# Int8 linear layer of a transformer kernel: rounding, transposes and product by halves of the tokens, casts placed earlier, second half scaled on ScalarE

## The chip, the cores and the metric

The kernel runs on one core of a Trainium2 chip. The metric is the device time of one execution in microseconds, lower is better.

## What is computed

The reference is four layers, each of an attention and a feed-forward part with a layernorm ahead and a residual sum behind. It works on 16 sequences of 64 tokens with 128 features. The change lies in the feed-forward part of the second layer (counted from 0, layer 1), an int8 product, cut here to what matters:

```python
def _xla_quantized_matmul(x2d, weight_q, weight_scale):
    amax = jnp.max(jnp.abs(x2d), axis=-1, keepdims=True)
    x_scale = jnp.maximum(amax, EPS) / 127.0
    x_q = jnp.clip(jnp.round(x2d / x_scale), -128, 127).astype(jnp.int8)
    acc = jax.lax.dot_general(x_q, weight_q, (((1,), (1,)), ((), ())), preferred_element_type=jnp.int32)
    return acc.astype(jnp.float32) * x_scale * weight_scale[None, :]
...
x = x + _L1_xattn_ref(_layernorm(x, axis=-1), ctx_1024, ctx_1024, ...)     # channel attention
x = x + _L1_ffn_ref(_layernorm(x, axis=-1), weight_q, weight_scale, bias)  # product above, + bias
x = x + _L2_xattn_ref(ctx_1024, ctx_1024, _layernorm(x, axis=-1), ...)     # deformable attention
```

## The kernel before

The 1024 tokens are eight tiles of 128 (tokens on the partitions, 128 features along a row). The residual stream is `x_tm`, its layernorm `h_tm`, the transposed layernorm `h_fm`. There are no loops at run time: each stage writes out, engine by engine, a fixed list of instructions with waits on semaphores, and the lists of one engine follow each other in the order of the source. So the order on an engine is the order in the text, and an instruction behind a wait stands until the wait is met.

The stages around the change, in order:

- `channel_attention(2)` (from L1118). On TensorE the last product (L1172) is two halves of 64 matmuls; VectorE stands at `wait_ge(y_ps, k + 1)` (L1198), adds each half to `x_tm` (L1202) and takes statistics (L251).
- `int8_linear(3)` (L1294 to L1389). A layernorm of all tiles: VectorE makes five tiles of `h_tm` (L277), ScalarE three (L292). VectorE casts the integer weights to bf16 (`wq8b`, L1312) and the identity matrix (`ident_b`, L1313), finds the largest magnitude of each token (L1315), the scale `xs` and its reciprocal (L1316, L1317), multiplies (L1318), rounds by adding and taking away a large constant (L1319), and clips into bf16 (`xq`, L1320). TensorE transposes the eight tiles into PSUM bank 4 (L1354), ScalarE copies them out in one instruction (`xT`, L1380), TensorE multiplies tile by tile by `wq8b` into banks 2 and 3 (L1360) and counts up `y_ps` after each half. Meanwhile VectorE adds the bias to `x_tm` (L1321). Then for each half k it multiplies the product by the token's scale into `y` (L1325), by the weight's scale (L1330), adds it to `x_tm` (L1331) and takes statistics. Half 0's layernorm is begun by `first_norm.moments` (L336, L338), its square root is ScalarE's (`first_norm.root`, L342 and L344), and its factors and two of its four tiles are done on VectorE (L349, L350, L365) between L1325 and L1330 of half 1; ScalarE does the two other tiles (L358). `second_norm` does the same for half 1.
- Around the int8 product, TensorE fills waits with matmuls whose result nobody reads (`stay_busy`, L241). Behind the product it transposes nine blocks of another layer's weights (L1367) into banks 6, 7 and 5, makes the last layer's keys in banks 0 and 1 (L1371), runs two more `stay_busy` matmuls and then transposes half 0 of `h_tm` (`first_norm.turn`, L376). ScalarE copies the weights' transposes out (L1383), then does the root, the keys' first half (L1255), its tiles of `h_tm` (L358), the keys' second half, and `h_fm` (L382).
- `deformable(4)` starts from `h_fm`: queries (L1457, L1465) and offsets (L1477) on TensorE, copies on ScalarE (L1548, L1554), positions on VectorE (L1577 and on), first for half 0 and then for half 1.

`dve_link` lets VectorE wait for the end of the instruction just issued. `REST` counts DMAs of inputs, all issued at the kernel's start.

## Time and profile before

| | us |
|---|---|
| median of 3 runs | 476.1 |
| the 3 runs | 476.1, 476.27, 471.72 |
| profiled execution, its own time | 471.51 |
| profiled execution, span of its trace | 469.7 |
| PE, DVE, ACT, POOL busy in the span | 393.7, 363.0, 247.9, 110.7 |
| mean granted TensorE clock | 0.967 |

The span runs from the first to the last instruction. PE is TensorE (PEld its weight loads), DVE is VectorE, ACT is ScalarE, POOL is GpSimd. Times within the trace count from the start of the span. A timeline line gives start, duration, engine, source line, operation, tensors, shapes and count; merged instructions stand on one line, and in brackets is how long the engine had been idle and what released it. In the chain of waits a line gives start, duration and what was running; its pieces do not overlap.

### The profile page before, as it was taken

How to read it: one execution, taken by the hardware profiler on the slowest of the kernel's cores; microseconds unless marked ns; L12 is line 12 of the kernel's file. 1: busy time of each engine (PE TensorE's matmuls, PEld its weight loads, DVE VectorE, ACT ScalarE, POOL GpSimd, SP SyncE). 2: the span in 40 equal slices, each digit the busy share in tenths (PEclk: the TensorE clock that was granted, in tenths of full speed). 3: DMA queues.
4: the chain of work that ended last, by engine and by line, in shares of the span. 5: the costliest groups of instructions: out<-in, count | busy, mean ns of one | idle time of the engine just before them, and what ended most of it. 6: DMA issues, size and time to landing. Idle time of an engine off the chain costs nothing.

```text
span 469.7 us, 8627 instructions
## 1 busy us (share of the span) xinstructions
PE 393.7 (84%) x3391; PEld 259.2 (55%) x3391; DVE 363.0 (77%) x805; ACT 247.9 (53%) x429; POOL 110.7 (24%) x95
## 2 busy tenths in 40 slices
PE   4999889999999988786887888899999995678056
PEld 1656556566666667553454446575667763553045
DVE  3799656648544587889878898999898789777985
ACT  3764853324223334457787884855866334435931
POOL 3200000005990001006995345210410133000000
PEclk9999999999999999989999999999999998979659
DMA  7880000000000000026000003000000000000001
GB/s 241 354 298 3 2 1 0 2 0 1 0 1 0 1 3 2 0 98 262 2 1 0 3 1 68 1 1 2 0 1 1 2 0 1 3 0 0 1 0 46
DMA packets 11084, 16.51 MB, mean 35 GB/s; under 512 B 5274, under 2 KB 9764, under 8 KB 10148
## 3 DMA queue, kind: packets, MB, share of 16 engines
q1 hardware_dynamic: 10756, 15.17, 9.2%
q10 hardware_dynamic: 288, 0.79, 0.5%
q8 instruction: 27, 0.44, 0.4%
q14 instruction: 13, 0.11, 0.1%
HBM read 15.43 MB, written 0.52 MB: 34 GB/s over the span
## 4 chain that ended last, share of the span: by engine, by line
PE 48%; DVE 32%; ACT 11%; issue 6%; DMA 1%; POOL 1%; DVEq 0%; ACTq 0%
PE ps L808 7%; PE ps L813 7%; PE ps L847 7%; PE ps L2075 4%; PE ps L241 3%; DVE arena L613 2%; PE ps L2065 2%; DVE arena L616 2%; DVE arena L1862 2%; PE ps L1714 2%; DVE stats L251 2%; PE ps L2102 1%; DVE arena L635 1%; DMA ctx_fm<-in_ctx_fm 1%; PE ps L2617 1%
## 5 line engine op out<-in xcount | busy, mean ns | idle before, releaser
L926 DVE SCALAR_TENSOR_TENSOR arena<-ps,cols,arena 128x512 f32<-128x512 f32 x40 | 29.8, 750 | 42.3 <-PE ps L813 38.0
L822 ACT ACTIVATE arena<-ps,cols 128x512 f32<-128x512 f32 x40 | 27.4, 687 | 63.9 <-PE ps L808 63.9
L241 PE MATMUL ps<-const 128*128 128x256 f32 x152 | 40.1, 412 | 7.4 <-ACT arena L2658 4.4
L847 PEld LDWEIGHTS ps<-weights,arena 128*128 128x128 f32 x320 | 38.5, 192 | 8.1 <-issue 8.0
L1862 DVE TENSOR_SCALAR arena<-ps 128x512 f32<-128x512 f32 x56 | 36.4, 684 | 7.3 <-PE ps L1700 3.5
L847 PE MATMUL ps<-weights,arena 128*128 128x128 f32 x320 | 39.2, 276 | 0.2 <-DVE x_tm L915 0.2
L241 PEld LDWEIGHTS ps<-const 128*128 128x128 f32 x152 | 29.8, 205 | 16.4 <-ACT arena L2658 4.7
L813 PE MATMUL ps<-h_fm,weights 128*128 128x512 f32 x80 | 37.7, 593 | 0.7 <-DVE arena L926 0.7
L808 PE MATMUL ps<-h_fm,weights 128*128 128x512 f32 x80 | 37.7, 594 | 0.6 <-ACT h_fm L382 0.6
L2065 PE MATMUL ps<-h_fm,weights 128*128 128x512 f32 x64 | 30.3, 606 | 2.7 <-ACT arena L2443 1.8
L1700 PE MATMUL ps<-l2buf,picks_b 128*128 128x256 bf16 x160 | 25.5, 275 | 6.5 <-DVE arena L1862 4.7
L2075 PEld LDWEIGHTS ps<-weights,arena 128*128 128x128 f32 x256 | 29.4, 192 | 2.6 <-issue 2.6
L2075 PE MATMUL ps<-weights,arena 128*128 128x128 f32 x256 | 30.0, 275 | 0.9 <-DVE x_tm L2287 0.9
L813 PEld LDWEIGHTS ps<-h_fm,weights 128*128 128x128 f32 x80 | 15.1, 190 | 20.2 <-issue 18.2
L1714 PE MATMUL ps<-arena,kexp 128*32 128x320 f32 x256 | 20.5, 438 | 5.3 <-ACT l2buf L1805 3.9
L1021 POOL TENSOR_TENSOR wn<-wn,winv 128x1152 f32<-128x1152 f32 x1 | 2.1, 2127 | 88.8 <-DVE winv L1011 88.8
L2443 ACT ACTIVATE arena<-ps 128x512 f32<-128x512 f32 x32 | 18.0, 597 | 9.2 <-PE ps L2065 9.1
L915 DVE SCALAR_TENSOR_TENSOR x_tm<-ps,arena,x_tm 128x128 f32<-128x128 f32 x80 | 22.4, 342 | 0.3 <-DVE stats L251 0.2
L1700 PEld LDWEIGHTS ps<-l2buf,picks_b 128*128 128x128 bf16 x160 | 12.6, 99 | 16.9 <-DVE arena L1862 10.0
L2065 PEld LDWEIGHTS ps<-h_fm,weights 128*128 128x128 f32 x64 | 11.2, 189 | 17.7 <-issue 10.2
L808 PEld LDWEIGHTS ps<-h_fm,weights 128*128 128x128 f32 x80 | 13.7, 191 | 10.4 <-issue 9.6
L2226 POOL TENSOR_TENSOR arena<-arena 128x1024 f32<-128x1024 f32 x5 | 11.5, 2298 | 31.7 <-DVE arena L2325 31.7
(391 smaller groups left out, 880.5 us busy)
## 6 DMA issues: line engine op xcount, KB each, us to landing
weights<-in_moe_w SPq DMA_DIRECT2D x2, 2048.0 KB, 9.9
weights<-in_moe_w SPq DMA_DIRECT2D x3, 1280.0 KB
l2buf<-in_picks SPq DMA_DIRECT2D x1, 1664.0 KB, 7.9
rows<-in_rows SPq DMA_DIRECT2D x1, 1024.0 KB, 13.1
x_tm<-in_x SPq DMA_DIRECT2D x2, 256.0 KB, 5.0
ctx_fm<-in_ctx_fm ACTq DMA_DIRECT2D x1, 512.0 KB, 5.7
ctx_tm<-in_ctx SPq DMA_DIRECT2D x1, 512.0 KB, 14.0
mats<-in_mats SPq DMA_DIRECT2D x1, 512.0 KB, 14.4
```

Source lines behind the costliest of these rows:

```text
L241: PE.matmul(ps[:, bank, 0:256], ident, const[:, 0:256], start=True, stop=True)
L808: PE.matmul(ps[:, k, :], w1[:, e, P * k:P * k + P], h_fm[:, t], start=True, stop=True)\
L813: PE.matmul(ps[:, 2 + k, :], w2[:, e, P * k:P * k + P], h_fm[:, t], start=True, stop=True)\
L822: AC.activation(silu[:, k, :], ps[:, k, :], ACT.Silu, bias=bias_col(0, e, k)).then_inc(silu_ok, 1)
L847: ins = PE.matmul(ps[:, 4 + u % 2, P * t:P * t + P], glu[:, u % 2, k, P * t:P * t + P], w3[:, e, k, :], start=(k == 0), stop=(k == 1))
L915: ins = V.scalar_tensor_tensor(out=x_tm[:, j], in0=ps[:, 4 + u % 2, P * t:P * t + P], scalar=gates[:, j, e:e + 1], in1=x_tm[:, j], op0=ALU ...
L926: V.scalar_tensor_tensor(out=glu[:, u % 2, k, :], in0=ps[:, 2 + k, :], scalar=bias_col(1, e, k), in1=silu[:, k, :], op0=ALU.add, op1=ALU.m ...
L1700: ins = PE.matmul(ps[:, m % 3, 256 * i:256 * i + 256], picks_b[:, 2 * c + i, :], ixm[:, hg, 256 * half:256 * half + 256], start=True, stop ...
L1714: ins = PE.matmul(ps[32 * hl:32 * hl + 32, 4 + par, 0:NK * S], kvc[:, j, 4 * hg + hl, :], hats[:, u % 2, NK * hl:NK * hl + NK, S * (2 * i ...
L1862: V.tensor_scalar(hat_rows(u, c), ps[:, m % 3, :], 0.0, 1.0, ALU.max, ALU.min).then_inc(near_ok, 1)
L2065: PE.matmul(ps[:, n % 3, :], m2w1[:, e, P * k:P * k + P], h_fm[:, 0:T2], start=True, stop=True)\
L2075: ins = PE.matmul(at_ps, hid[:, e % 2, k, P * j:P * j + P], m2w2[:, e, k, :], start=(k == 0), stop=(k == 3))
```

## The change

The two casts are issued in the channel attention, ahead of VectorE's wait for the first half of its last product. The clip (L1320), the transposes, the copy out of PSUM and the product are each issued in two halves of four tiles; the second half's transposes go to bank 5. ScalarE, which before had only the copy to do here, waits for the product's second half and multiplies it, tile by tile, by the token's scale `xs`; VectorE keeps this step for the first half alone, and ahead of L1330 of half 1 it waits for ScalarE (`xT_ok` at 6: two copies and four scalings).

```diff
@@ channel_attention, VectorE
                 dve.wait_ge(dve_chain, biased)
+                dve.wait_ge(rest_in, REST)
+                V.tensor_copy(wq8b[:], wq8[:])
+                V.tensor_copy(ident_b[:], ident)
                 for k in range(2):
                     t = slice(4 * k, 4 * k + 4)
                     dve.wait_ge(y_ps, k + 1)
@@ int8_linear, VectorE
-                dve.wait_ge(rest_in, REST)
-                V.tensor_copy(wq8b[:], wq8[:])
-                V.tensor_copy(ident_b[:], ident)
                 wait_h_tm(dve)
...
-                V.tensor_scalar(xq, t, -128.0, 127.0, ALU.max, ALU.min).then_inc(xq_ok, 1)
+                for k in range(2):
+                    r = slice(4 * k, 4 * k + 4)
+                    V.tensor_scalar(xq[:, r], t[:, r], -128.0, 127.0, ALU.max, ALU.min).then_inc(xq_ok, 1)
...
-                    dve.wait_ge(y_ps, k + 1)
-                    dve_link(V.tensor_tensor(y[:, r], ps[:, 2 + k, :].rearrange("p (j c) -> p j c", j=4),
-                                             over(xs[:, r], 2, D), ALU.mult))
+                    if k == 0:
+                        dve.wait_ge(y_ps, 1)
+                        dve_link(V.tensor_tensor(y[:, r], ps[:, 2, :].rearrange("p (j c) -> p j c", j=4),
+                                                 over(xs[:, r], 2, D), ALU.mult))
                     if k == 1:
                         first_norm.factors(dve)
                         first_norm.apply_on_dve(dve, (0, 1))
+                        dve.wait_ge(xT_ok, 6)
@@ int8_linear, TensorE
-                pe.wait_ge(xq_ok, 1)
-                for j in range(NT):
-                    ins = PE.transpose(tp[:, P * j:P * j + P], xq[:, j], ident_b[:])
-                ins.then_inc(xT_ps, 1)
-                pe.wait_ge(xT_ok, 1)
                 for k in range(2):
+                    pe.wait_ge(xq_ok, k + 1)
+                    tp = ps[:, 4 + k, :].bitcast(BF16)
+                    for j in range(4):
+                        ins = PE.transpose(tp[:, P * j:P * j + P], xq[:, 4 * k + j], ident_b[:])
+                    ins.then_inc(xT_ps, 1)
+                for k in range(2):
+                    pe.wait_ge(xT_ok, k + 1)
                     for j in range(4):
                         i = 4 * k + j
@@ int8_linear, ScalarE
-                act.wait_ge(xT_ps, 1)
-                AC.activation(xT, ps[:, 4, :].bitcast(BF16), ACT.Copy).then_inc(xT_ok, 1)
+                for k in range(2):
+                    act.wait_ge(xT_ps, k + 1)
+                    AC.activation(xT[:, 512 * k:512 * k + 512], ps[:, 4 + k, :].bitcast(BF16)[:, 0:512], ACT.Copy)\
+                        .then_inc(xT_ok, 1)
+                act.wait_ge(y_ps, 2)
+                for j in range(4, NT):
+                    AC.activation(y[:, j], ps[:, 3, P * (j - 4):P * (j - 4) + P], ACT.Copy, scale=xs[:, j:j + 1])\
+                        .then_inc(xT_ok, 1)
```

The buffers `wq8b` and `ident_b` are declared ahead of the channel attention for it; nothing else changes.

## Rows read from the trace of the kernel before

**Rows 1.** The chain of waits, 192 to 206 us: start, duration, what.

```profile
...
192.87 0.20 DVE ident_b L1313
...
196.66 0.70 DVE arena L1320
...
198.07 1.03 ACT arena L1380
...
199.65 0.70 DVE arena L1325
...
203.95 0.19 DVE rstd L349
...
204.36 0.89 ACT h_tm L358 x2
...
```

**Rows 2.** VectorE in order of time: start, duration, instruction, [idle before, releaser].

```profile
...
185.19 1.40 DVE L1202 TENSOR_TENSOR x_tm<-x_tm,ps 64x512 f32<-64x512 f32 x2 [2.38 <-PE ps L1172]
...
192.72 0.22 DVE L1312 CAST wq8b<-wq 128x128 bf16<-128x128 int32 x1
192.85 0.22 DVE L1313 CAST ident_b<-const 128x128 bf16<-128x128 f32 x1
192.99 1.21 DVE L1315 TENSOR_REDUCE arena<-h_tm 128x8 f32<-128x1024 f32 x1
...
197.27 1.22 DVE L1321 TENSOR_TENSOR x_tm<-x_tm,rows 128x1024 f32<-128x1024 f32 x1
...
203.15 0.17 DVE L338 TENSOR_SCALAR rstd<-mv 128x4 f32<-128x4 f32 x1
203.23 0.68 DVE L1325 TENSOR_TENSOR arena<-ps,arena 128x512 f32<-128x512 f32 x1
...
209.81 0.43 DVE L1577 TENSOR_TENSOR o_fm<-o_fm,const 128x256 f32<-128x256 f32 x1 [0.22 <-ACT o_fm L1554]
...
```

**Rows 3.** TensorE in order of time, same columns.

```profile
...
191.13 5.02 PE L241 MATMUL ps<-const 128*128 128x256 f32 x22 [1.01 <-ACT rstd L289]
197.41 0.62 PE L1354 MATMUL ps<-ident_b,arena 128*128 128x128 bf16 x8 [1.26 <-DVE arena L1320]
199.15 0.62 PE L1360 MATMUL ps<-wq8b,arena 128*128 128x128 bf16 x8 [1.12 <-ACT arena L1380]
199.60 1.80 PE L1367 MATMUL ps<-const,wn 128*128 128x128 f32 x9
...
203.99 1.03 PE L241 MATMUL ps<-const 128*128 128x256 f32 x4
205.29 0.66 PE L376 MATMUL ps<-const,h_tm 128*128 128x128 f32 x4 [0.27 <-ACT h_tm L358]
...
```

**Rows 4.** ScalarE in order of time, same columns.

```profile
...
191.55 1.26 ACT L292 ACTIVATE h_tm<-x_tm,shift,rstd 128x128 f32<-128x128 f32 x3 [0.47 <-DVE shift L274]
...
203.35 0.20 ACT L344 ACTIVATE rstd<-rstd 128x4 f32<-128x4 f32 x1 [1.28 <-DVE rstd L338]
203.47 0.67 ACT L1255 ACTIVATE k_fm<-ps,cols 128x512 f32<-128x512 f32 x1
...
```

**Rows 5.** ScalarE by line and shape, 190 to 216 us: busy, mean ns.

```profile
...
L358 ACT ACTIVATE h_tm<-x_tm,shift,rstd 128x128 f32<-128x128 f32 x4 | 1.7, 484 | 0.2 <-DVE shift L350 0.2
...
L1383 ACT ACTIVATE wT<-ps 128x512 f32<-128x512 f32 x2 | 1.2, 597 | 1.5 <-PE ps L1367 1.5
...
L1383 ACT ACTIVATE wT<-ps 128x128 f32<-128x128 f32 x1 | 0.3, 273 | 0.0
...
```

**Rows 6.** VectorE by line and shape, 190 to 216 us, same columns.

```profile
...
L1594 DVE TENSOR_SCALAR o_fm<-o_fm 128x256 f32<-128x256 f32 x1 | 0.3, 295 | 0.0
...
```

**Rows 7.** Windows: length, busy time and instructions by engine, granted clock, DMA.

```profile
...
199.00:200.00 1.00, 0.85 (x12) 0.86 (x13) 0.35 (x1) 0.09 (x1) 0.00 (x0) 0.97 0.00 0
200.00:201.00 1.00, 1.00 (x7) 1.00 (x6) 0.97 (x2) 0.60 (x1) 0.00 (x0) 0.50 0.10 25
203.00:204.00 1.00, 1.00 (x4) 0.43 (x3) 0.93 (x5) 0.65 (x2) 0.00 (x0) 0.82 0.00 0
...
```

More of the change, by code:

```diff
@@ L1222, in _ @@
                 keys_values_l2_blocks(act, (0, 1), 6)
-        channel_attention(2)
         wq8b = sb("wq8b", [P, P], BF16)
         ident_b = sb("ident_b", [P, P], BF16)
+        channel_attention(2)
         l3_keys = (sem("L3_k_ps"), sem("L3_k_sb"))
@@ L1341, in _ @@
             def _(pe):
-                tp = ps[:, 4, :].bitcast(BF16)
                 pe.wait_ge(chan_added, 2)
```

## The prediction

> **What bounds the kernel now.** I read the chain of waits first, because a change of some 20 instructions in 8627 can only matter where it lies on the chain, and it does: between 192.8 and 206 us the chain runs through the very lines that are edited [rows 1]. The reader is to see that it changes its engine at almost every step: VectorE prepares the int8 operand, TensorE transposes, ScalarE copies 1.03 us, TensorE multiplies, VectorE scales, ScalarE takes the root. No engine is full there; each waits for another's whole block. TensorE is idle for 1.26 us ahead of the transposes and for 1.12 us between them and the product [rows 3], VectorE has nothing to do between the end of its bias addition (197.27 + 1.22 = 198.49) and the product's first half at 199.65 [rows 1, 2]. So finer blocks can shorten this. The timelines of the single engines then say how far each step may move before something else is late, and the windows say at which level TensorE's clock stood.
>
> **The casts.** In the channel attention VectorE is idle for 2.38 us ahead of L1202, waiting for TensorE [rows 2]. The casts take 0.22 us each and cost nothing there; the inputs they read have long landed, since VectorE passes the same wait much earlier in the kernel, for the weights' scales. What they give back is less than their 0.35 us. ScalarE finishes its last tile of `h_tm` at 191.55 + 1.26 = 192.81 [rows 4]; the reduction starts at 192.99, behind the casts [rows 2]. A start about 0.1 us behind what it waits for makes it 192.91. **Gain 0.08 us**, at least nothing, at most 0.18 (without a delay). In the following I keep the times of before and add this 0.08 at the end.
>
> **The clip in halves.** 1024 elements take 0.70 us [rows 1] and 256 take 0.295 [rows 6], so 512 take 0.43. The instructions overlap by about 0.08 us (the bias addition starts at 197.27 while the clip ends at 197.36), so the halves end at 197.09 and 196.66 + 0.35 + 0.43 = 197.44. The whole costs VectorE 0.08 us; the bias addition ends at 198.57 in place of 198.49 and is still ahead of the product.
>
> **Transposes, copy, product.** Eight bf16 transposes take 0.62 us and follow each other by (199.60 - 199.15)/8 = 0.056 us, so four take 0.40 [rows 3]. TensorE started 0.05 us behind the clip. First half: 197.15 to 197.55. ScalarE's copy of 512 columns takes 0.60 [rows 5], its start 0.04 behind: 197.59 to 198.19. Second half: transposes ready by 197.90, copy behind the first with the 0.08 us overlap that the pair of L358 shows (0.89 for two of 0.484) [rows 1, 5]: 198.11 to 198.71. The product's first half starts 0.05 behind its copy, at 198.24, and VectorE started 0.50 behind the product [rows 1, 3]: 198.74 in place of 199.65. **Gain 0.91 us at L1325.** The second half starts at 198.76, its issue is over at 198.98, and the weights' transposes, which started at 199.60, follow then: TensorE's list is 0.62 us ahead.
>
> **Scaling on ScalarE.** It can begin at 198.76 + 0.40 + 0.04 = 199.20. The trace has no 128x128 activation with a scale per partition alone. The bounds are 0.273 us for a plain copy out of PSUM and 0.484 for one with both a scale and a bias [rows 5]; I take the middle, 0.38, since it has one of the two operands. Four with the overlap take 3 x 0.30 + 0.38 = 1.3 us (0.85 to 1.7). ScalarE is free at 200.5, then copies the weights' transposes: 2 x 0.60 + 0.27, less the overlaps, about 1.3, and the dummy root 0.2, to 202.0 (202.4 at the upper bound). VectorE's L338 ended at 203.15 + 0.17 = 203.32 and now at 202.41 [rows 2]. So the added work and the added wait (`y_ps` at 2, behind which stand the weights' copies, the root, the keys' copy and half 0's `h_tm`) are hidden in ScalarE's 1.28 us of idle time ahead of L344 [rows 4]; without that cover they would cost up to 1.3. VectorE's new wait for ScalarE is for something done 2 us earlier.
>
> The Trainium skill's "ScalarE: Activation LUTs", section "Rules for kernel authors", speaks against this move: multiplications belong on VectorE, which is faster for each element. The rows agree on the price (0.68 us on VectorE [rows 2] against my 1.3), and by the rule the kernel would lose if ScalarE were late at the root; by the rows it is not.
>
> **Root and half 0's layernorm.** Before, the root came at 203.35 [rows 4], but VectorE was held by L1325 of half 1 until 203.91 [rows 2] and took the reciprocal at 203.95 [rows 1]. Now the root starts at 202.44, ends at 202.64, and VectorE, without that L1325, goes on at 202.69: 1.26 us earlier. ScalarE's tiles (L358) could start at 204.36 - 1.26 = 203.10. ScalarE copies the keys' first half in between (0.67 us, L1255); these keys were ready by 203.43 and are 0.62 earlier, 202.81 at the latest, which puts L358 at 203.1 to 203.45.
>
> **What is late next.** TensorE. Its list (weights' transposes, keys, `stay_busy`) ended at 203.99 + 1.03 = 205.02, and it waited only 0.27 us before it transposed half 0 at 205.29 [rows 3]. The list is 0.62 ahead, so these transposes start at 204.40 at the earliest; `h_tm` is there at about 204.1 to 204.4. The gain here is 0.62 + 0.27 = 0.89, plus 0.08 of the casts: **about 1.0 us**. VectorE's half 1 is 1.3 us ahead and is no longer late anywhere: its second root waits for ScalarE's queue, which follows the transposes.
>
> **To the end.** Behind this point each step waits for another step: VectorE's first work on the positions (L1577) stood 0.22 us for ScalarE's copy [rows 2], and the rest of the deformable attention hangs on it. [...] So the 1.0 us goes through to the end: 471.5 - 1.0 = 470.5 by the profiled execution, whose span of 469.7 has 1.8 us around it. That execution lies near the lowest of the three timings, 471.72; the two others are 476.1 and 476.3. The median is at the upper level, so there I expect 476.1 - 1.0 = **475.1**.
>
> **The rivals.**
>
> First, the clock. TensorE's granted clock was at the full 2.4 GHz until about 199.9 us and at half, 1.2 GHz, until about 203.4 (0.97, then 0.50, then 0.82 of full in the windows of 1 us) [rows 7]. Ahead of the fall TensorE had been idle from 196.15 to 199.15 but for the 0.62 us of transposes [rows 3]. In the changed kernel the idle time there is shorter, 196.15 to 197.07 and two small gaps, so the fall may not come. Then 3.4 us at half level are full, TensorE's list is up to 1.7 us further ahead, and the turn is bound by ScalarE's tiles instead: a gain of 1.26 + 0.08 = 1.3 us, 474.8. For it speaks the shorter gap; against it, that a fall not seen in half of the idle stretches may come or go between executions. The Trainium skill's "TensorE: Matmul & The Clock Gate", section "HAM oscillation — how this bites in real kernels", has idle gaps throttle the clock again, and would make this the likelier outcome; the trace agrees so far as its fall follows the longest gap of this stage.
>
> Second, the other side: the fall comes all the same but later, over the transposes, queries and offsets of half 0, from 205.29 to 209.31, where TensorE is on the path. Some 2.8 us of it are TensorE's (ScalarE has about 1.2), and at half level they take up to 1.5 us more. Against the gain of 1.3 this makes it slower by 0.2 us, 476.3. It decides where the fall begins behind 204 us. Against it: TensorE's first idle time after that is short.
>
> Third, the halves do nothing: if the bf16 copy of 512 columns costs almost what that of 1024 does (1.03), the two end at 199.5 and only the casts' 0.08 and the 0.25 from the freed VectorE remain: 475.8. The f32 copy at 0.60 speaks against it.
>
> Fourth, the level. Three timings spread over 4.6 us, 1% of the kernel, with nothing changed. Whatever sets it, the median of some runs of the changed kernel can fall at the lower level, 471.6 - 1.0 = 470.6, which would be read as faster by more than 1%.
>
> **How the numbers follow.** About 1% is what a measurement of this kernel can tell from no change. Gain of about 1.0 at the level of the median: 0.42. The same gain with the clock kept, 474.8: 0.20. The lower level, 470.3 to 470.7: 0.26. Nothing gained by the halves: 0.07. The fall moved, 476.3: 0.05. The chance of faster by over 1% is almost all that of the lower level, 0.24; of slower by over 1%, 0.03, for a level above those seen. The rest, 0.73, is no change that can be told. The range goes from 470.0, a little under the lower level with the largest gain, to 476.6, a little above the other side.
>
> **What the profile would show.** The reduction L1315 0.1 us earlier; the casts ahead of L1202, with its start unmoved; ScalarE's two copies 0.6 us each, back to back; L1325 once, 1.0 us earlier; four activations of 0.38 us that nobody waits for; the reciprocal L349 1.3 us earlier; L376 1.0 us earlier, now waiting for TensorE's own list; L1577 1.0 us earlier, and the same distance to the end. I would be wrong by more than the range if the new schedule turned a later stage's clock from full to half, or if ScalarE reached the root late: L344 would then start behind 202.5 us with no idle time ahead of it.

## The result

The changed kernel takes 472.5 us in the median (470.7 to 473.6, 20 executions), the kernel before 474.9 us beside it (471.5 to 476.3, 20 executions): a ratio of 0.9958 with a 95% interval of 0.9938 to 0.9977, or 2.0 us less (1.1 to 2.9). It is faster, by less than the 1% that was taken as the bound of what can be told. The forecast was 475.1 in a range of 470.0 to 476.6, with 1.0 us less than the kernel before.

The profiled execution of the changed kernel took 473.6 us, with a span of 471.8 against 469.7 before. So in this one pair of profiles the changed kernel is the longer one, and the two must be compared piece by piece. In the whole document "the stage" is the stretch from TensorE's first matmul of the channel attention's last product (L1172) to VectorE's first instruction on the positions (L1577 before, L1584 after), each start read in a timeline. It takes 26.85 us before (182.96 to 209.81) and 25.48 after (185.77 to 211.25).

VectorE in the changed kernel, in order of time; these answer to [rows 2]:

```profile
...
185.54 0.18 DVE L1197 CAST wq8b<-wq 128x128 bf16<-128x128 int32 x1
185.65 0.22 DVE L1198 CAST ident_b<-const 128x128 bf16<-128x128 f32 x1
187.93 1.40 DVE L1205 TENSOR_TENSOR x_tm<-x_tm,ps 64x512 f32<-64x512 f32 x2 [2.07 <-PE ps L1172]
...
195.67 1.22 DVE L1312 TENSOR_REDUCE arena<-h_tm 128x8 f32<-128x1024 f32 x1
...
199.35 0.76 DVE L1319 TENSOR_SCALAR arena<-arena 128x512 bf16<-128x512 f32 x2
200.03 1.22 DVE L1320 TENSOR_TENSOR x_tm<-x_tm,rows 128x1024 f32<-128x1024 f32 x1
201.43 0.69 DVE L1325 TENSOR_TENSOR arena<-ps,arena 128x512 f32<-128x512 f32 x1 [0.18 <-PE ps L1361]
...
204.93 0.17 DVE L338 TENSOR_SCALAR rstd<-mv 128x4 f32<-128x4 f32 x1
205.37 0.18 DVE L349 RECIPROCAL rstd<-rstd 128x4 f32<-128x4 f32 x1 [0.27 <-ACT rstd L344]
...
211.25 0.42 DVE L1584 TENSOR_TENSOR o_fm<-o_fm,const 128x256 f32<-128x256 f32 x1 [0.22 <-ACT o_fm L1561]
...
```


The casts stand in the wait ahead of L1205 (2.07 us are left of 2.38). From L1172 on, the reduction comes 9.90 us later in place of 10.03 (192.99 - 182.96), the product's first half is taken up at 15.66 in place of 16.69, and the reciprocal of half 0 at 19.60 in place of 20.99.

ScalarE of the same execution, answering to [rows 4], with the same columns:

```profile
...
200.28 1.09 ACT L1382 ACTIVATE arena<-ps 128x512 bf16<-128x512 bf16 x2 [2.03 <-PE ps L1355]
201.85 1.14 ACT L1386 ACTIVATE arena<-ps,arena 128x128 f32<-128x128 f32 x4 [0.49 <-PE ps L1361]
...
205.13 0.20 ACT L344 ACTIVATE rstd<-rstd 128x4 f32<-128x4 f32 x1 [0.91 <-DVE rstd L338]
205.25 0.67 ACT L1255 ACTIVATE k_fm<-ps,cols 128x512 f32<-128x512 f32 x1
205.81 0.86 ACT L358 ACTIVATE h_tm<-x_tm,shift,rstd 128x128 f32<-128x128 f32 x2
...
```

And TensorE, answering to [rows 3]:

```profile
...
199.84 0.73 PE L1355 MATMUL ps<-ident_b,arena 128*128 128x128 bf16 x8 [0.94 <-DVE arena L1319]
200.93 0.89 PE L1361 MATMUL ps<-wq8b,arena 128*128 128x128 bf16 x8 [0.36 <-ACT arena L1382]
201.65 1.15 PE L1368 MATMUL ps<-const,wn 128*128 128x128 f32 x9
...
204.36 1.03 PE L241 MATMUL ps<-const 128*128 128x256 f32 x4
206.73 0.66 PE L376 MATMUL ps<-const,h_tm 128*128 128x128 f32 x4 [1.35 <-ACT h_tm L358]
...
```


The two copies take 1.09 us together, the four scalings 1.14, and ScalarE still waits 0.91 us for VectorE ahead of the root (1.28 before). TensorE's list of weights, keys and idle matmuls is over at 204.36 + 1.03 = 205.39; then it waits 1.35 us for the layernorm's tiles. Before it waited 0.27, because its list was slow: the clock stood at half from 199.9 to 203.4 [rows 7]. In the changed kernel's profile it is full over the whole stage, and at half elsewhere. Windows of the changed kernel, as in [rows 7]: the granted clock is the third number from the end.

```profile
...
49.00:53.00 4.00, 4.00 (x59) 3.30 (x60) 2.21 (x8) 2.91 (x7) 0.00 (x0) 0.57 0.02 4
...
96.00:101.00 5.00, 5.00 (x27) 4.64 (x27) 2.50 (x6) 0.00 (x0) 0.00 (x0) 0.66 0.00 0
...
200.00:220.00 20.00, 14.15 (x106) 8.47 (x105) 17.09 (x53) 13.31 (x31) 3.05 (x5) 1.00 0.52 208
...
```


These two falls, at 49 and 96 us, lie in the first layer, whose code is the same in both kernels, and the time from the start to L1172 is 185.77 us against 182.88 to 184.21 in the profiles that have none or one of them. That is the 2.8 us which hide the stage's gain of 1.37 in this pair of profiles.

The last piece, from the next experts' first matmul to the end, differs too: 174.76 us before, 175.43 after. Its code is the same in both, and TensorE's clock is at half in several stretches of it in every profile, at other times and for other lengths. Behind 394 us it is at half until about 398 in the kernel before and until about 404 in the changed one, which puts the changed one 0.4 us behind; the fall behind it is the longer one in the kernel before (about 411.5 to 418 us, 414.5 to 418 in the changed one) and evens this out. What is left arises at ten idle matmuls (L241) ahead of the last product. The clock is at half over the first of them, until about 456 us before and 459 after. TensorE in the kernel before, in order of time (a matmul of f32 counts as two here):

```profile
...
452.40 6.32 PE L241 MATMUL ps<-const 128*128 128x256 f32 x20 [4.36 <-ACT arena L2658]
...
```

And in the changed kernel:

```profile
...
453.61 7.19 PE L241 MATMUL ps<-const 128*128 128x256 f32 x20 [4.36 <-ACT arena L2665]
...
```

TensorE's next step follows them at once, and VectorE waits for it, 1.35 us before and 2.21 after. The same group takes 6.05 to 7.55 us in the other profiles. The last piece takes 175.2 us or more in all profiles but that of the kernel before, those of kernels with whole blocks included. So the halves are not what lengthens it; whether the change has a part in it, through the moments at which steps arrive, is not shown.

### The profile page after: what moved, and what is told of

Its sections match the earlier page's. It is cut to its first block, busy times and chain, and to the rows that moved or that the text cites. A ratio compares the mean times of both kernels' runs of the same rounds, so it can differ in the third digit from the quotient of the medians.

```text
span 471.8 us, 8631 instructions
## 1 busy us (share of the span) xinstructions
PE 396.5 (84%) x3391; PEld 261.7 (55%) x3391; DVE 362.6 (77%) x805; ACT 248.7 (53%) x434; POOL 110.7 (23%) x95
## 4 chain that ended last, share of the span: by engine, by line
PE 49%; DVE 30%; ACT 11%; issue 7%; DMA 1%; POOL 1%; POOLq 0%; DVEq 0%; ACTq 0%
PE ps L847 7%; PE ps L808 7%; PE ps L813 7%; PE ps L2082 4%; DVE arena L613 2%; PE ps L241 2%; PE ps L2072 2%; DVE arena L616 2%; DVE arena L1869 2%; PE ps L1721 2%; DVE stats L251 2%; PE ps L2109 1%; DVE arena L635 1%; DMA ctx_fm<-in_ctx_fm 1%; PE ps L2624 1%
## 5 line engine op out<-in xcount | busy, mean ns | idle before, releaser
L241 PE MATMUL ps<-const 128*128 128x256 f32 x152 | 40.8, 418 | 7.4 <-ACT arena L2665 4.4
L847 PEld LDWEIGHTS ps<-weights,arena 128*128 128x128 f32 x320 | 40.1, 198 | 8.1 <-issue 8.0
L847 PE MATMUL ps<-weights,arena 128*128 128x128 f32 x320 | 40.8, 283 | 0.2 <-DVE x_tm L915 0.2
L241 PEld LDWEIGHTS ps<-const 128*128 128x128 f32 x152 | 30.2, 207 | 16.4 <-ACT arena L2665 4.7
L2082 PEld LDWEIGHTS ps<-weights,arena 128*128 128x128 f32 x256 | 29.4, 192 | 2.6 <-issue 2.6
L2082 PE MATMUL ps<-weights,arena 128*128 128x128 f32 x256 | 30.0, 275 | 0.9 <-DVE x_tm L2294 0.9
```

Source lines behind the costliest of these rows:

```text
L241: PE.matmul(ps[:, bank, 0:256], ident, const[:, 0:256], start=True, stop=True)
L847: ins = PE.matmul(ps[:, 4 + u % 2, P * t:P * t + P], glu[:, u % 2, k, P * t:P * t + P], w3[:, e, k, :], start=(k == 0), stop=(k == 1))
L2082: ins = PE.matmul(at_ps, hid[:, e % 2, k, P * j:P * j + P], m2w2[:, e, k, :], start=(k == 0), stop=(k == 3))
```

## The experiments

All ratios are to the kernel before, run beside each of the three groups on that group's chip (medians 475.2, 473.9 and 474.2 us, 35 executions each; the first group, e, ran on one chip, the other two, f and g, on another). Each kernel was timed 12 times and profiled once. I read each profile in the same pieces, named by what ends them: the first matmul of L1172; the end of the stage; VectorE's first instruction on the weights ("hats") of the sampled positions, L1862 in the kernel before; TensorE's first matmul of the next experts, L2065; the end of the span. All are in us.

```
kernel            span   start to  the    to the first  to the next  to the
                         L1172     stage  hat (L1862)   experts      end
before            469.7  182.96    26.85  7.06          78.07        174.76
changed           471.8  185.77    25.48  7.06          78.06        175.43
e1_casts          473.4  183.33    28.34  8.67          77.66        175.40
e2_halves         469.8  183.29    25.93  7.05          78.14        175.39
e3_scale          473.1  183.27    28.11  8.67          77.65        175.40
e4_busy           475.8  182.88    30.63  8.97          77.94        175.38
f1_after_fill     469.3  183.12    25.48  7.05          78.10        175.55
f2_before_fill    472.9  183.39    26.86  7.05          78.09        177.51
f3_scale3         471.1  184.00    26.53  7.05          78.16        175.36
f4_fill_more      469.1  183.10    25.47  7.06          78.10        175.37
g1_no_busy        472.1  183.94    27.73  7.48          77.75        175.20
g2_best           471.2  184.21    26.26  7.05          78.09        175.59
g3_best_fill      470.5  183.77    26.26  7.06          78.07        175.34
g4_after_again    471.6  185.63    25.47  7.05          78.10        175.35
```

The column "to the first hat" holds the second half's queries, "to the next experts" the deformable attention. Where no clock falls in them, these two repeat to 0.1 us, and so does the stage between kernels with the same work in it. The first and the last column do not: the first follows the falls at 49 and 96 us (none 182.9 to 183.4, at 96 alone 183.8 to 184.2, both 185.6 and 185.8), the last has falls in all profiles.

### The parts alone: e1_casts, e2_halves, e3_scale

**e1_casts** is the kernel before with the casts moved:

```diff
@@ channel_attention, VectorE
+                dve.wait_ge(rest_in, REST)
+                V.tensor_copy(wq8b[:], wq8[:])
+                V.tensor_copy(ident_b[:], ident)
@@ int8_linear, VectorE
-                dve.wait_ge(rest_in, REST)
-                V.tensor_copy(wq8b[:], wq8[:])
-                V.tensor_copy(ident_b[:], ident)
```

> The kernel before with the two casts alone moved ahead of the wait in the channel attention. I measure the stage from the first matmul of the channel attention's last product to VectorE's first instruction on the positions: 26.85 us before, 25.48 us in the changed kernel. Theory A (the gain is the sum of the path's own steps): the stage takes 26.75 to 26.80 us, the median moves by less than 0.2 us. Rival B (moving the casts takes their whole 0.35 us off the path): 26.5 us.

Measured: 473.7 us, ratio 0.9987 (0.996 to 1.0014). Up to half 0's transposes the path is 0.11 us shorter (22.22 us behind L1172 in place of 22.33), as theory A has it and not by rival B's 0.35. But the stage takes 28.34 us and the next piece 8.67: both 1.6 us longer. TensorE's timeline of e1_casts says why:

```profile
...
197.66 0.62 PE L1351 MATMUL ps<-ident_b,arena 128*128 128x128 bf16 x8 [1.21 <-DVE arena L1317]
199.40 0.62 PE L1357 MATMUL ps<-wq8b,arena 128*128 128x128 bf16 x8 [1.12 <-ACT arena L1377]
199.85 1.15 PE L1364 MATMUL ps<-const,wn 128*128 128x128 f32 x9
...
205.55 0.66 PE L376 MATMUL ps<-const,h_tm 128*128 128x128 f32 x4 [1.96 <-ACT h_tm L358]
206.89 1.44 PE L1454 MATMUL ps<-h_fm,mats 128*128 128x512 f32 x2 [0.69 <-ACT h_fm L382]
208.26 2.03 PE L1462 MATMUL ps<-mats,h_fm 128*64 128x128 f32 x16
210.02 1.54 PE L1474 MATMUL ps<-q_fm,woff 128*64 128x256 f32 x8
...
```

And its windows, where the granted clock is again the third number from the end:

```profile
...
207.00:210.00 3.00, 3.00 (x18) 1.93 (x20) 1.57 (x11) 0.87 (x3) 0.00 (x0) 0.59 0.61 158
...
214.00:217.00 3.00, 2.76 (x10) 1.27 (x11) 2.79 (x9) 0.87 (x2) 0.00 (x0) 0.57 1.00 426
...
```


TensorE had waited 1.96 us ahead of the transposes. The clock then fell to half at about 207 us, over the queries (L1454, L1462) and the offsets (L1474), and again at 214 over the second half's. L1462 takes 2.03 us where it took 1.14. Both falls are on the path, unlike that of [rows 7]. e3_scale shows the same two falls at the same places. That the kernel before does this as well in many of its executions, and that its one profile happened to show another case, is what the timings below suggest; no profile of it shows it. Two more things stand in this timeline. The idle times ahead of the int8 transposes (1.21 us) and ahead of the product (1.12) are those of the kernel before, and yet the clock stays full at the product: the weights' transposes (L1364) take 1.15 us where they took 1.80. And TensorE's list is done early, so that it waits 1.96 us and not 0.27; the transposes still start where the layernorm's tiles allow it.

**e2_halves** is the kernel before with the clip, transposes, copy and product by halves, as in the change's diff; VectorE scales both halves.

> The kernel before with the clip, transposes, copy and product by halves alone; VectorE scales both halves and the casts stand where they did. Theory A: the product's first half is 0.9 us earlier and the stage takes 25.9 to 26.0 us (0.9 us less), most of the whole gain; the median falls by about 0.9 us. Rival B (most of the gain comes from the clock that no longer falls in this stage, and from VectorE's freed step): the halves alone give under 0.5 us.

Measured: 472.4 us, ratio 0.9958 (0.9935 to 0.9981), the whole gain of the change within the intervals. The product's first half is taken up 0.92 us earlier (15.77 behind L1172 in place of 16.69), half 0's transposes start 0.92 earlier (21.41), the stage takes 25.93, so rival B (under 0.5 us) falls. TensorE waits 1.69 us ahead of them, and the clock stays full, as TensorE's timeline of e2_halves shows in the unchanged durations of the queries and offsets:

```profile
...
204.70 0.66 PE L376 MATMUL ps<-const,h_tm 128*128 128x128 f32 x4 [1.69 <-ACT h_tm L358]
206.04 1.13 PE L1463 MATMUL ps<-h_fm,mats 128*128 128x512 f32 x2 [0.69 <-ACT h_fm L382]
207.10 1.15 PE L1471 MATMUL ps<-mats,h_fm 128*64 128x128 f32 x16
208.02 1.08 PE L1483 MATMUL ps<-q_fm,woff 128*64 128x256 f32 x8
...
```


**e3_scale** is the kernel before with the scaling alone:

```diff
+                act.wait_ge(y_ps, 2)
+                for j in range(4, NT):
+                    AC.activation(y[:, j], ps[:, 3, P * (j - 4):P * (j - 4) + P], ACT.Copy, scale=xs[:, j:j + 1])\
+                        .then_inc(xT_ok, 1)
```

(and `dve.wait_ge(xT_ok, 5)` in place of VectorE's own step for half 1).

> The kernel before with the second half's scaling on ScalarE alone; the transposes and the copy stay whole and the casts stand where they did. Theory A: VectorE takes the reciprocal 0.3 us earlier, TensorE's list allows 0.27, the stage takes about 26.55 us and the median falls by 0.3 us. Rival B (ScalarE comes late to the root): the stage takes 26.85 us or more and ScalarE has no idle time ahead of the root.

Measured: 473.1 us, ratio 0.9973 (0.9945 to 1.0002). Half 0's transposes start 0.33 us earlier (22.00), and then the two falls cost what they cost in e1_casts. ScalarE still waits 1.17 us ahead of the root, so rival B (ScalarE late) falls too. The three parts give 0.11, 0.92 and 0.33 us at the transposes, together 1.36; the changed kernel has 1.37 (20.96 in place of 22.33). So the path's gain is additive, and two thirds are the halves. TensorE waited 1.62 us ahead of half 0's transposes in e3_scale, with falls, and 1.69 in e2_halves, without.

### The clock over the path: e4_busy, f1_after_fill, f2_before_fill, f4_fill_more, g1_no_busy, g4_after_again

```diff
@@ e4_busy, on the kernel before
-                stay_busy(pe, 7, 5)
+                stay_busy(pe, 12, 5)
...
                 ins.then_inc(xT_ps, 1)
+                stay_busy(pe, 4, 5)
                 pe.wait_ge(xT_ok, 1)
```

> The kernel before with nine more matmuls that nobody reads: five ahead of the int8 transposes and four between them and the product, which fill TensorE's two idle times and delay nothing. Theory A (the path alone counts): the turn of half 0 waits for the layernorm's tiles, not for TensorE, so even without a fall of the clock the stage takes 26.8 to 26.9 us in the profile and the median does not move by over 0.3 us. Rival B (in many executions the clock falls over the path of this stage, which one profiled execution need not show, and the changed kernel is faster by 2 us and not by 1 because it avoids that): the median falls by 0.6 to 1.2 us and the slowest executions by 1 to 2.5 us.

Measured: 476.4 us, ratio 1.0042 (1.0015 to 1.0069). The expectation rested on a wrong size. I had read 0.22 us for one such matmul, from lines that count each f32 matmul twice; it takes 0.45. TensorE's timeline of e4_busy:

```profile
...
191.05 7.17 PE L241 MATMUL ps<-const 128*128 128x256 f32 x32 [1.01 <-ACT rstd L289]
198.06 0.61 PE L1354 MATMUL ps<-ident_b,arena 128*128 128x128 bf16 x8
198.51 1.95 PE L241 MATMUL ps<-const 128*128 128x256 f32 x8
200.29 0.61 PE L1361 MATMUL ps<-wq8b,arena 128*128 128x128 bf16 x8
...
```


The five are over only at 198.2 and the four at 200.5, so the transposes and the product are late and VectorE takes up the product 1.22 us later (17.91). The run says nothing for or against rival B, except that in its profile a TensorE without idle time around the product did not prevent the later falls: its wait ahead of half 0's transposes was 1.95 us, and the clock fell at 206, again over the path.

The next two kernels put four such matmuls (0.45 us each) into waits they fit into:

```diff
@@ f1_after_fill on the changed kernel, f2_before_fill on the one before; deformable, TensorE
+                stay_busy(pe, 1, 3)
                 first_norm.wait_turned(pe)
...
                 offsets(0)
+                stay_busy(pe, 2, 3)
                 second_norm.turn(pe, 4)
+                stay_busy(pe, 1, 3)
                 second_norm.wait_turned(pe)
```

> The changed kernel with four more matmuls that nobody reads, put into waits of TensorE that stand on the path: one of 0.45 us behind half 0's transposes (wait 0.69), two ahead of half 1's transposes (wait 1.33), one behind them (0.69). Each fits its wait, so without the clock the stage stays at 25.5 us. Theory C (falls of the clock over the queries and offsets are what the median holds beyond the path's own steps, and the changed kernel has few of them left): the median is equal to or at most 0.5 us below the changed kernel's 472.5. Rival D (the falls depend on nothing in this stage): equal too; the next run tells them apart.

> The kernel before with the same four matmuls. Theory C: the falls over the queries and offsets, which cost 1.5 us in the profiles of two kernels with the old blocks, become rarer; the median falls by 0.8 to 1.5 us from 475.2, to about that of the changed kernel plus the 1.4 us of the path (473.9). Rival D: the median does not move by more than 0.3 us.

Measured: f1_after_fill 471.2 us, ratio 0.9951 (0.9925 to 0.9978), stage 25.48; f2_before_fill 473.5 us, ratio 0.9994 (0.9963 to 1.0026; one of its twelve executions took 801 us), stage 26.86. In the timeline of TensorE in f2_before_fill the idle matmuls (two records for one matmul) fit as meant:

```profile
...
205.72 0.66 PE L376 MATMUL ps<-const,h_tm 128*128 128x128 f32 x4 [1.95 <-ACT h_tm L358]
206.22 0.60 PE L241 MATMUL ps<-const 128*128 128x256 f32 x2
207.07 1.13 PE L1457 MATMUL ps<-h_fm,mats 128*128 128x512 f32 x2 [0.25 <-ACT h_fm L382]
208.12 1.15 PE L1465 MATMUL ps<-mats,h_fm 128*64 128x128 f32 x16
...
```


TensorE had waited the same 1.95 us as in e1_casts, and the clock stayed full over the queries (L1465 at 1.15 us). And with a full clock and whole blocks the stage takes 26.86 us, just what the kernel before took with its clock at half over TensorE's list: that fall cost the path nothing. But the median moved by 0.5 and not by the 0.8 to 1.5 of theory C, and the interval includes no change. One of the eleven normal executions took over 475 us, against 13 of the 35 of the kernel before beside it, which is too few to settle it. As a test of theory C the run is inconclusive.

f1_after_fill's median was expected at most 0.5 us below the changed kernel's 472.5 and is 1.3 below it. Beside it, on the same chip, the kernel before also had its lowest median, and the interval of its ratio (0.9925 to 0.9978) contains that of the changed kernel's (0.9938 to 0.9977), so no gain of the four matmuls is shown.

**f4_fill_more** has `stay_busy(pe, 4, 4)` in place of `stay_busy(pe, 2, 4)` ahead of half 0's transposes as well.

> The kernel of f1_after_fill with two more such matmuls (0.9 us) ahead of half 0's transposes, in the changed kernel's wait of 1.35 us there. Theory C: stage of 25.5 us, no fall of the clock from the product to the end of the offsets, the median equal to or up to 0.5 us below that of f1_after_fill. Rival (in executions in which the clock falls at the product, TensorE's list is late and these two come on the path): the slowest executions are 0.5 to 1 us above those of f1_after_fill.

Measured: 472.3 us, ratio 0.9966 (0.9941 to 0.9991), stage 25.47, slowest execution 473.3 against 472.8. The median is 1.1 us above that of f1_after_fill where 0 to 0.5 below was expected, and the slowest execution 0.5 above, the lower edge of what the rival has. In the profile no step is late; a gain is not seen.

**g1_no_busy** takes idle matmuls away where f4 adds them:

```diff
                 pe.wait_ge(kv_ok, 8)
...
-                stay_busy(pe, 2, 4)
                 first_norm.turn(pe, 4)
```

> The changed kernel without the two idle matmuls ahead of half 0's transposes, so that TensorE waits there for 2.3 us in place of 1.35; no step of the path changes. Theory C (the kernel before was often late because the clock fell over the queries and offsets of both halves, behind a wait of 1.96 us; the changed kernel is not because its wait is shorter): the falls come back, in the profile or in the timings, as executions about 2.7 us above the lowest; the median is 0.5 to 2 us above that of the changed kernel run beside it. Rival D (the length of that wait has nothing to do with it): median within 0.4 us of the changed kernel's, stage 25.5 us.

> The changed kernel once more, beside the three above on the same chip. Expected: 25.5 us in the stage unless its profile shows a fall of the clock there, the median 1.5 to 2.5 us below that of the kernel before, no execution above 474.

Measured: g1_no_busy 471.6 us, ratio 0.9978 (0.9946 to 1.001); the changed kernel beside it, g4_after_again, 472.7 us, ratio 0.9957 (0.9936 to 0.9979), stage 25.47. The median of g1_no_busy is not above but 1.1 us below, which contradicts that part of theory C's expectation. The other part came out in kind: seven of its twelve executions took 470.4 to 471.9 us and five took 473.9 to 475.8, up to 5.4 above its lowest where 2.7 was expected, and its profile, of an execution near 474, has a fall of the clock back over the path of half 0. TensorE in g1_no_busy:

```profile
...
204.90 0.66 PE L376 MATMUL ps<-const,h_tm 128*128 128x128 f32 x4 [2.21 <-ACT h_tm L358]
206.24 2.08 PE L1463 MATMUL ps<-h_fm,mats 128*128 128x512 f32 x2 [0.69 <-ACT h_fm L382]
208.25 2.03 PE L1471 MATMUL ps<-mats,h_fm 128*64 128x128 f32 x16
210.01 1.97 PE L1483 MATMUL ps<-q_fm,woff 128*64 128x256 f32 x8
...
```


Nothing on the path was changed against the changed kernel, TensorE only waits 2.21 us in place of 1.35, and the stage takes 27.73 in place of 25.47. So a fall of the clock over this path costs over 2 us, and executions above the changed kernel's slowest came back with the removal of two idle matmuls.

The length of this one wait does not decide it, though. Over the fourteen profiles:

| wait ahead of half 0's transposes, us | fall over the path | none |
|---|---|---|
| 0.27 to 1.35 | - | before (its fall lies ahead, at the product), changed, f1, f4, g2, g3, g4 |
| 1.62 to 2.40 | e1 (1.96), e3 (1.62), e4 (1.95), g1 (2.21) | e2 (1.69), f2 (1.95), f3 (2.40) |

The falls come only with the longer waits, but in four of seven, and a wait of 2.40 us had none where one of 1.62 had one. What else decides is open.

The timings point the same way. Of 124 executions of the kernel before (one odd one of 598 us left out) 52 took over 475 us, and its levels are about 471.5, 473.5 and 475.8; of 32 executions of the changed kernel none took over 473.7, although its lowest (470.5) is only 0.7 below the other's (471.2). The path's 1.37 us does not account for this: it would only bring the 52 down to 473.7 and more, where the changed kernel has none. The 52 are also executions with a lower clock: of the 42 of them beside the experiments 36 have a mean granted clock of 0.950 to 0.957, while those under 472 have 0.963 to 0.971. In which piece of the kernel the clock fell there, the timings don't tell.

### ScalarE's cover: f3_scale3

```diff
                 act.wait_ge(y_ps, 2)
+                for again in range(2):
+                    for j in range(4, NT):
+                        spare = arena[:, 4096 + 512 * again + P * (j - 4):4096 + 512 * again + P * (j - 3)]
+                        AC.activation(spare, ps[:, 3, P * (j - 4):P * (j - 4) + P], ACT.Copy, scale=xs[:, j:j + 1])
                 for j in range(4, NT):
```

> The changed kernel whose ScalarE scales the second half three times (twice into a spare part of the arena that nobody reads), 2.1 us more work in the same place. Theory A (ScalarE had 0.9 us idle ahead of the root, and this is all the cover there is): the root is 1.2 us later, the stage takes 26.7 us if the clock holds, the idle time ahead of the root is gone, and the median is over 1 us above the changed kernel's. Rival: the scaling is on no path at all and the stage stays at 25.5 us.

Measured: 473.1 us, ratio 1.001 (0.998 to 1.004), the stage 26.53 us.

ScalarE in f3_scale3:

```profile
...
200.08 2.18 ACT L1388 ACTIVATE arena<-ps,arena 128x128 f32<-128x128 f32 x8 [0.49 <-PE ps L1361]
202.09 1.20 ACT L1390 ACTIVATE arena<-ps,arena 128x128 f32<-128x128 f32 x4
203.09 1.34 ACT L1393 ACTIVATE wT<-ps 128x512 f32<-128x512 f32 x3
204.21 0.32 ACT L342 ACTIVATE table<-table 128x1 f32<-128x1 f32 x1
204.30 0.32 ACT L344 ACTIVATE rstd<-rstd 128x4 f32<-128x4 f32 x1
...
```


The eight added activations put the last four off by 2.01 us (200.08 to 202.09). The root now starts with no idle time ahead of it, and the stage is 1.05 us longer: 2.01 - 1.05 = 0.96 us were covered, close to the 0.91 us of idle time that the changed kernel's profile shows ahead of L344. The rival, that the scaling is on no path at all, falls. The median lies 0.4 to 1.9 us above those of the changed kernel and f1_after_fill, not clearly by the 1 us expected. TensorE waits 2.40 us ahead of half 0's transposes here, and four of the twelve executions took 475.4 to 477.5 us, though the profiled one has no fall there.

### A further step: g2_best, g3_best_fill

```diff
@@ int8_linear, on the changed kernel
-                dve_link(V.tensor_tensor(t, h_tm[:], over(inv, 2, D), ALU.mult))
-                dve_link(V.tensor_scalar(t, t, MAGIC, -MAGIC, ALU.add, ALU.add))
                 for k in range(2):
                     r = slice(4 * k, 4 * k + 4)
+                    dve_link(V.tensor_tensor(t[:, r], h_tm[:, r], over(inv[:, r], 2, D), ALU.mult))
+                    dve_link(V.tensor_scalar(t[:, r], t[:, r], MAGIC, -MAGIC, ALU.add, ALU.add))
                     V.tensor_scalar(xq[:, r], t[:, r], -128.0, 127.0, ALU.max, ALU.min).then_inc(xq_ok, 1)
-                dve_link(V.tensor_tensor(x_tm[:], x_tm[:], over(row("L1_ffn_bias"), 1, NT), ALU.add))
+            @block.gpsimd
+            def _(pool):
+                wait_h_tm(pool)
+                G.tensor_tensor(x_tm[:], x_tm[:], over(row("L1_ffn_bias"), 1, NT), ALU.add).then_inc(bias_ok, 1)
```

VectorE waits for `bias_ok` ahead of L1333, and ScalarE copies the ninth block of weights behind L358 in place of ahead of the root. g3_best_fill adds the four matmuls of f1_after_fill.

> The changed kernel with the multiplication and the rounding by halves as well, the addition of the bias on GpSimd, which is idle, and ScalarE's third copy of weights behind its tiles of the layernorm. The first half of the clip ends 0.78 us earlier by VectorE's rows. Theory A: the product's first half and the root follow it, the stage takes 24.7 to 24.9 us, the median is 0.7 us below the changed kernel's. Rival (ScalarE's queue, now with less idle time than the 0.9 us it had, comes late to the root): 25.1 to 25.4 us.

> The kernel of g2_best with the four matmuls of f1_after_fill in TensorE's waits on the path. Expected: the same stage time, 24.7 to 24.9 us, a median equal to or up to 0.5 us below that of g2_best, and the narrowest spread of all kernels.

Measured: g2_best 474.2 us, ratio 0.9998 (0.9974 to 1.0022; one of its twelve executions took 597 us); g3_best_fill 472.6 us, ratio 0.9982 (0.9955 to 1.0008); both with a stage of 26.26 us, 0.8 longer than the changed kernel's and not 0.7 shorter. VectorE in g2_best:

```profile
...
194.10 1.22 DVE L1313 TENSOR_REDUCE arena<-h_tm 128x8 f32<-128x1024 f32 x1
195.36 1.17 DVE L1314 TENSOR_SCALAR arena<-arena 128x8 f32<-128x8 f32 x1
196.56 0.20 DVE L1315 RECIPROCAL arena<-arena 128x8 f32<-128x8 f32 x1
...
```

GpSimd in g2_best:

```profile
...
194.14 2.36 POOL L1381 TENSOR_TENSOR x_tm<-x_tm,rows 128x1024 f32<-128x1024 f32 x1 [14.29 <-ACT h_tm L292]
```


L1314 works on 8 elements a partition and took 0.17 us in the kernels whose bias stays on VectorE. Here it takes 1.17, and ends at 196.53, just behind the end of GpSimd's addition (194.14 + 2.36 = 196.50). The profile of g3_best_fill has the same: 1.17 us, ending 0.03 us behind GpSimd. The reduction ahead of it ran beside GpSimd at its usual 1.22. I read this as 1.0 us that the bias on GpSimd cost VectorE on the path. By this estimate the stage without it would have been at about 25.3 us, near the changed kernel's, which is also short of the 24.8 I had expected. VectorE waited 0.71 us for the product there. A version with the halves but without GpSimd was not run, so the cause is inferred from the times and not shown by a run. g3_best_fill's executions spread over 4.3 us (470.9 to 475.1), f1_after_fill's over 2.2: the narrowest spread, which was expected of it, it does not have. No kernel here beats the changed one beyond its interval; f1_after_fill has the lowest ratio.

## Why the prediction was right, and where it was off

**The casts.** 0.08 us forecast, 0.13 measured at the reduction (9.90 in place of 10.03) and 0.11 at the transposes. Right; the remaining 0.2 of the casts lay beside ScalarE's last tile, as argued.

**The halves.** 0.91 us forecast at L1325, 0.92 measured in e2_halves. Each term holds: the two clips together 0.76 (0.78 forecast), the two copies 1.09 (1.12). The third rival, in which they do nothing, falls.

**The scaling on ScalarE.** 1.3 us forecast, 1.14 measured (0.368 each, between the bounds of 0.273 and 0.484). It is hidden: ScalarE waits 0.91 us ahead of the root, and f3_scale3 shows that the cover ends there. The Trainium skill's "ScalarE: Activation LUTs", section "Rules for kernel authors", puts multiplications on VectorE as the faster engine for each element; the trace agrees on the direction (1.14 us against 0.68 on VectorE), and the move still gains 0.33 us, because one engine was on the path and the other was not.

**Root and reciprocal.** 1.34 us earlier with the casts forecast, 1.39 measured.

**What is late next.** Here the main line was off in mechanism and in size. I had TensorE's list bound the transposes (a gain of 1.0) and the kept clock as the first rival (1.3). In all profiles of the changed kernel and of those with the halves the clock stays full at the product, TensorE waits for the tiles (1.35 us in the changed kernel), and the changed kernel gains 1.37: the rival's case and its size, not the forecast's. But the reason that the rival gave, the shorter idle time ahead of the product, is not borne out. The clock stays full there in e1_casts, e3_scale and f2_before_fill too, which keep the whole blocks and both idle times (1.21 to 1.27 and 1.12 us). Of the fourteen profiles only that of the kernel before has this fall. I had taken something that one execution showed as a property of the kernel. What the halves would gain in an execution that has it, no run shows.

**To the end.** Right for the two pieces behind the stage, which are the same to 0.1 us where no clock falls (7.06, 78.1 us). Not right for the last one: the distance to the end was to stay the same, and it is 174.76 us before and 175.43 after, by falls of the clock that I had not looked at. This fits the lowest executions, which differ by 0.7 us and not by 1.37.

**The other side.** The second rival had the fall of the clock move over the queries of half 0, at 1.5 us, and gave this 0.05 for the changed kernel. The mechanism exists, with that price (1.60 us for half 0 in e1_casts), and it comes in a pair, with 1.61 for half 1, of which 0.4 are given back in the following piece: 2.8 us together. But the forecast placed it in the changed kernel, and the runs show it with the old blocks, and with the halves only where two idle matmuls are taken out (g1_no_busy). I had asked what the change does to the one fall that the profile shows, and put the 4.6 us between the timings down to "whatever sets it", without asking whether the levels came in part from this very path.

**The median.** The forecast's 475.1 was 476.1 - 1.0. Over 20 executions the kernel before has a median of 474.9, so 1.2 of the 2.6 us between forecast and result are the base of three timings; 0.4 is the path (1.37 in place of 1.0); the other 1.0 (0.6 by the ratio, whose gain is 2.0 and not 2.4) is what the profiles of single executions don't hold. The interval of that gain, 1.1 to 2.9 us, includes the path's 1.37, so the medians alone don't show that there is more. That the result lies in the forecast's range is in part luck: the range spans two levels, 471 and 476, and 472.5 is the median of none of the cases that were given a chance (the nearest are 470.6 and 474.8). The falls over the path, seen in three of the five profiles with whole blocks (e1_casts, e3_scale, e4_busy; not in the kernel before and f2_before_fill) and in none of the changed kernel's two, and the missing top level fit a further gain in sign and size. That the top level is made of these falls is not shown execution by execution, since only one of each kernel's is profiled, and f2_before_fill, meant to show it by the median, did not settle it. There are other sources of 2 us and more in the same code: f2's profile has a piece at the end of 177.5 us in place of 175.4, and the falls at 49 and 96 us cost 2.8.

## What to carry to other kernels

Where the chain changes its engine at every step, cut the block that is handed over, and sum the gain from starts and durations: the three parts added up to 0.01 us. When the timings of one kernel stand on separate levels, find out what the levels are before forecasting a change of their size: one profile shows one of the cases, and a fall of the clock that it shows can be absent from the next. And an idle time of TensorE ahead of a critical run of matmuls may be a risk of its own: here falls over that run came only behind waits of 1.6 us and more, in four profiles of seven, and each cost over 1.5 us. That shortening the wait is worth more than the path says is likely by the missing slow executions, and not shown by a median.

## What was not expected of the hardware

A VectorE instruction on 8 elements a partition took 1.17 us in place of 0.17 while GpSimd ran an addition over 128x1024 f32, and ended with it, in both profiles that have this addition; the reduction ahead of it was not slowed. Ten idle matmuls took 6.05 to 7.55 us by where TensorE's clock stood at half, ahead of a product that was on the path. And the places where TensorE's clock fell to 1.2 GHz moved between executions in code that is the same in all kernels: at 49 and 96 us in both profiles of the changed kernel, at 96 alone in four others, at neither in the rest.
